# Attention operands of a tuned layer kernel as two fp16 halves, kept in memory after the first batch

## The reference

```
q, k, v = x@Wq+bq, x@Wk+bk, x@Wv+bv        # 16 heads of 128; q times 128**-0.5
q, k    = rotary(q), rotary(k)
attn    = softmax(q k^T under a causal mask)
x1      = layernorm(x + concat(attn v) @ Wo + bo)
y       = silu(x1@Wg * sg) * (x1@Wu * su)  # Wg, Wu, Wd int8, 1024 wide
out     = layernorm(x1 + (y@Wd) * sd)
```

## Time and profile before

| | |
|---|---|
| median of 3 runs | 1857.92 us (1856.61 to 1859.83) |
| the profiled execution | 1852.92 us, its span 1851.1 us |
| PE, PEld busy | 95%, 76% |
| DVE, ACT, POOL busy | 85%, 79%, 75% |
| TensorE granted clock, mean | 0.991 |

### The profile page before, as it was taken

The page is one execution under the profiler, slowest core; times in us unless marked ns, Lnnn a source line. Parts: engine busy times, 40 slices in busy tenths (PEclk is TensorE's granted clock), DMA queues, the critical chain, the costliest instruction groups (busy, mean ns, idle before and its releaser), DMA issues. The chain is left out here.

```text
span 1851.1 us, 33747 instructions
## 1 busy us (share of the span) xinstructions
PE 1755.6 (95%) x10464; PEld 1409.7 (76%) x10464; DVE 1564.9 (85%) x3748; ACT 1463.9 (79%) x2658; POOL 1394.8 (75%) x1293
## 2 busy tenths in 40 slices
PE   6899999999999999999999999999999999899997
PEld 4677877777777777777777777777777777668886
DVE  6788888888888888988888888888888889867886
ACT  5788888888888888888888888888888888754443
POOL 4688877778777878888778878787888877624554
PEclk9899999999999999999999999999999999989999
DMA  3756565666665666576666655675666765540001
GB/s 93 165 116 113 111 139 117 122 131 129 118 119 120 142 120 115 114 157 119 120 122 117 138 111 116 141 141 121 119 114 116 156 141 109 104 99 12 24 24 35
DMA packets 638257, 210.01 MB, mean 113 GB/s; under 512 B 609408, under 2 KB 622208, under 8 KB 636672
## 3 DMA queue, kind: packets, MB, share of 16 engines
q1 hardware_dynamic: 614400, 165.91, 47.9%
q10 hardware_dynamic: 23680, 41.95, 7.9%
HBM read 48.40 MB, written 8.39 MB: 31 GB/s over the span
## 5 line engine op out<-in xcount | busy, mean ns | idle before, releaser
L863 DVE SCALAR_TENSOR_TENSOR planes<-S,recip,planes 128x128 f16<-128x128 f32 (+7 forms) x512 | 417.5, 815 | 113.0 <-ACT planes L665 111.3
L656 ACT ACTIVATE S<-p_row,neg_max 128x128 f32<-128x128 f32 (+7 forms) x512 | 381.5, 745 | 138.9 <-DVE neg_max L853 138.8
L665 ACT ACTIVATE planes<-S,recip 128x128 f16<-128x128 f32 (+7 forms) x512 | 378.9, 740 | 101.4 <-DVE recip L914 73.7
L427 POOL TENSOR_TENSOR swap<-swap,sin_t 128x512 f32<-128x512 f32 x256 | 331.5, 1295 | 166.0 <-ACT swap L673 164.9
L853 DVE CUSTOM_DVE_ANT_0 p_row<-S,mask_row 128x128 f32<-128x128 f32 (+7 forms) x512 | 387.0, 756 | 27.0 <-PE S L1123 26.4
L421 POOL TENSOR_TENSOR rot<-rot,swap 128x512 f32<-128x512 f32 x252 | 325.5, 1292 | 53.6 <-DVE rot L904 50.7
L673 ACT ACTIVATE swap<-S,bqk 64x512 f32<-64x512 f32 x512 | 350.8, 685 | 18.6 <-PE S L1141 5.8
L1123 PE MATMUL S<-QKA 128*128 128x512 f32 (+4 forms) x1152 | 261.9, 354 | 10.3 <-DVE planes L863 5.7
L1123 PE MATMUL S<-QKB 128*128 128x512 f32 (+4 forms) x1152 | 260.4, 353 | 0.4 <-DVE planes L863 0.3
L1074 PE MATMUL O<-PT,VA 128*128 128x512 f16 (+3 forms) x1152 | 215.4, 328 | 29.0 <-issue 25.5
L1074 PE MATMUL O<-PT,VB 128*128 128x512 f16 (+3 forms) x1152 | 214.9, 327 | 29.4 <-issue 27.0
(11 more groups left out here) (134 smaller groups left out, 2955.5 us busy)
## 6 DMA issues: line engine op xcount, KB each, us to landing
w_raw<-in_w_heads ACTq DMA_DIRECT2D x64, 256.0 KB, 2.9
wv_raw<-in_w_heads ACTq DMA_DIRECT2D x32, 256.0 KB, 3.4
PT<-planes SPq DMA_TRANSPOSE x512, 3.4
wo_raw<-in_wo_heads ACTq DMA_DIRECT2D x32, 256.0 KB, 2.6
attn_d<-resid ACTq DMA_DIRECT2D x4, 1024.0 KB, 6.3
x_raw<-in_x_cols SPq DMA_DIRECT2D x3, 1024.0 KB, 5.9
...
```

What stands on the lines that cost most here:

```text
L427: nc.gpsimd.tensor_tensor(swap[:, c, :], swap[:, c, :], sin_t[:, half], ALU.mult).then_inc(sin_done, 1)
L656: nc.scalar.activation(row_psum(n, s)[:, 0:cols], p_row[:, k % 2, 0:cols], ACT.Exp, bias=neg_max[:, s:s + 1], scale=-1.0, accum_out=row_su ...
L665: nc.scalar.activation(row_halves(n, s)[:, 0], row_psum(n, s)[:, 0:cols].rearrange("p (j q) -> p j q", q=P), ACT.Copy, scale=recip[:, s:s ...
L863: nc.vector.scalar_tensor_tensor(halves_of[:, 1], row_psum(n, s)[:, 0:cols].rearrange("p (j q) -> p j q", q=P), recip[:, s:s + 1], halves_ ...
```

## The change

fp32r goes from x, W, WV, QK, OT and WO; they become fp16 in two halves, scaled so that they lie well inside fp16's range. The scales are computed from the data, in this way: a maximum on DVE, a sum over partitions on PE (a matmul with ones), a reciprocal on DVE. For W, WV and WO that is done in the first batch only, one weight at a time, and the finished halves are stored to DRAM (w_d, wv_d, wo_d); from the second batch on they are loaded from there, with no work on them. What depends on x (V's bounds, biases, factors) is computed once a batch for all heads. In the first batch GpSimd also multiplies each raw weight by its scale. x is scaled by ACT and DVE in the first batch, by GpSimd in the others. From the second batch on ACT copies groups 0, 1 and 2 of V, scaled, as fp32 into v_sb, and GpSimd makes both halves; group 3 stays on ACT and DVE. Large loads and stores are cut in four pieces, and the weights have two buffers each. The sum of the output becomes a multiply and add (factor pv). The feed-forward part keeps fp32r.

```diff
-    xT = sb("xT", [P, 2, KT, N], F32R)
+    xT = at(AT_X, "xT", [P, 2, KT, N])                       # fp16; W, WV, QK, OT, WO likewise
 # SP: stores of the finished halves, first batch
+                    if n < 0 and s in (4, 7) or 0 <= n < H - 2 and s == 6:
+                        keep_w(n + 2 if n >= 0 else s // 7)
 ...
 # POOL
+                    if n >= H and n < HEADS - 1 and par == 0 and s in POOL_V0:     # {4: 1, 5: 2}
+                        v_halves(n_pair(n, par), POOL_V0[s])
+                    if n >= H - 1 and n < HEADS - 2 and par == 1 and s in POOL_V1: # {7: 0}
+                        v_halves(n_pair(n, par), POOL_V1[s])
-                    if s == 0 and n >= 1 and n + 2 < HEADS:
-                        w_low(n + 2, par, 0)
-                        w_low(n + 2, par, 1)
+                    if 0 <= n < H - 3 and s == 5:
+                        w_scale(n + 3)
+                    if 1 <= n < H - 2 and s == 3:
+                        w_low(n + 2, 0)
+                        w_low(n + 2, 1)
+                    if n % H == H - 3 and n < HEADS - H and s >= 6:
+                        b, half = n // H + 1, s - 6
+                        pool.wait_ge(x_scaled, 2 * b + 2)
+                        nc.gpsimd.tensor_scalar(halves(x_raw, None, half), halves(x_raw, None, half),
+                                                sx[:, b % 2:b % 2 + 1], None, ALU.mult).then_inc(x_up, 1)
+            def v_halves(pair, i):
+                whole, tiles = v_sb[:, i, :].rearrange("p (t c) -> p t c", t=2), slice(2 * i, 2 * i + 2)
+                k = 3 * (pair - H // 2) + i + 1
+                pool.wait_ge(v_hi, 4 * pair + i + 1)
+                pool.wait_ge(attended, n_att(2 * pair - 3, 1, 7))
+                nc.gpsimd.tensor_copy(V[pair % 2][:, 0, tiles, :], whole).then_inc(vp_hi, 1)
+                pool.wait_ge(vp_hi, k)
+                nc.gpsimd.tensor_tensor(V[pair % 2][:, 1, tiles, :], whole, V[pair % 2][:, 0, tiles, :],
+                                        ALU.subtract).then_inc(vp_lo, 1)
 # ACT
-            w_high(0, 0, 0)
-            x_high(0, 0)
+            w_high(0, 0)              # waits for W's scale
+            w_high(0, 1)
+            x_high(0, 0)              # waits for x's scale, which waits for all of x
+                    if H - 3 <= n < HEADS - 3 and s == 7:
+                        load_w_halves(n + 3)
+                if in_sb(pair, i):    # pair >= 8 and i < 3
+                    wait(act, vp_lo, 3 * (pair - H // 2 - 1) + i + 1)
+                    nc.scalar.activation(v_sb[:, i, :], X[:, :], ACT.Copy, scale=of_pair(v_up, pair)).then_inc(v_hi, 1)
+                    return
 # DVE
-                    if par == 1 and s == 5 and makes_v(n + 1):
-                        weigh((n + 3) >> 1)
+                    if 0 <= n < H - 3 and s == (1 if n else 2):
+                        weigh_w(n + 3)                      # a maximum over 128x512
+                    if 0 <= n < H - 3 and s == 4:
+                        scale_w(n + 3)                      # four small operations; take_w, one more, ahead
+                    if par == 0 and s == 1 and own and n // 2 + 1 < H // 2:
+                        scale_v(n // 2 + 1)                 # three small ones; take_v, two more, ahead
+                    if par == 1 and s == 5 and (n + 3) // 2 < H // 2:
+                        weigh_v((n + 3) // 2)
+                    if par == 1 and s == 2 and own and n < H:
+                        weigh_wo(n // 2)                    # a maximum over 128x512
+                    if par == 1 and s == 5 and own and n < H:
+                        scale_wo(n // 2)                    # two small ones; take_wo, one more, ahead
+                    if n % H == H - 4 and 0 < n < HEADS - H and s == 3:
+                        weigh_all(n // H + 1)
+                    if n % H == H - 3 and 0 < n < HEADS - H and s == 1:
+                        scale_x(n // H + 1)                 # for all heads of the next batch
+                if in_sb(pair, i):                          # value_low
+                    return
-                nc.vector.tensor_tensor(into, into, X[:, :], ALU.add).then_inc(added, 1)
+                stt(into, X[:, :], of_pair(pv, pair), into, ALU.mult, ALU.add).then_inc(added, 1)
 # PE
+                        v_free(pe, n_v(n, par, i) - 1)      # in_sb groups: waits for ACT's copy, not for DVE
```

705 lines of the change are left out of this document (504 added, 201 removed).

## The result

The changed kernel takes **1841.3 us** (median of 4 runs, 1839.9 to 1844.7), the kernel before on the same chip 1857.3 (4 runs, 1856.0 to 1859.8): ratio 0.992, 95% interval 0.990 to 0.994. That is 16 us faster where 55 were forecast.

A forecast was written before the change was run, and what follows sets the result against it. The prediction took PE to bound the kernel: 1851.1 - 85 (steady heads) + 14 (batch 0) + 7 (opening) + 8 (boundaries) = 1795 us of span, 1797 as a time, 1802 as the median. The range was 1758 to 1855.

The forecast's parts named there:

- the likeliest case: Whole kernel: the forecast itself holds, median 1802 us, own range 1780 to 1828, chance 0.50.
- So PE sets the pace, but nobody is far behind: Kernel before: PE, busy 95% of the span, bounds it; DVE, ACT and POOL follow at 40 to 44 of 50 us.
- fp16's 1.7 us: PE, every head: matmul columns at the fp16 instead of the fp32r rate save 1.7 us, bounds 1.5 and 2.0.
- The term of the steady heads: Heads 16 to 62: 23.0 us a head instead of 24.8, -85 us over 47 heads, bounds -66 and -108.
- the wait in slot 0: PE ahead of a head's first attend: the wait stays, mean 0.7 us a head against 1.0 before.
- the 0.2 put down for GpSimd: From batch 1 on: low half of chunk 1 just in time or slightly late behind V's halves, 0.2 us a head.
- Rival (B): Even runs: GpSimd's V halves make the low half of chunk 1 2 us late, +47 us, 1849 us; chance 0.20.
- Rival (D): POOL: fp16 operations cost more than fp32's, deciding from 15% dearer on, 1887 us at 20%; chance 0.13.
- Batch 0: First batch: DVE's added maxima and small operations lengthen 13 heads by 1.1 us each, +14 us, bounds -10 and +33.
- Opening: Before the first scores: maxima, small operations and two matmuls for the scales add 7 us, bounds 3 and 12.
- Boundaries: Between batches: POOL's scaling of x and DVE's small operations lose 3, 3 and 2 us, +8, bounds 0 and 20.
- signs of being wrong: PE waiting for POOL, POOL's fp16 rows off 0.61 and 1.29, batch 0 over 27 us a head, boundaries over 5 each.

The follow-up runs named there:

- 6: Kernel before with ACT's high parts of the weights cut to a few columns, later heads' weights stale: 1851.3 us, ratio 0.9997 to the kernel before.
- 10: Kernel before with the third product of every projection chunk left out, PE 1.85 us a head less: 1828.8 us, ratio 0.9855 to the kernel before.
- 11: Kernel before with both cuts, ACT's high parts of the weights and the third product of every chunk: 1819.2 us, ratio 0.9801 to the kernel before.
- 4: Changed kernel with a constant as the mask's factor instead of one read from SBUF, scores scaled wrongly: 1832.1 us, ratio 0.9889 to the kernel before.
- 5: Changed kernel with all V halves made on ACT and DVE again, GpSimd's part left out: 1844.9 us, ratio 0.996 to the kernel before.
- 17: Changed kernel with batch 0's bv copies on ACT, and later even heads' output projection in slot 2, V's last group in 4: 1857.6 us, ratio 1.0016.
- 12: Changed kernel with batch 0's weight maxima on DVE taken over four columns, scales no longer maxima: 1835.3 us, ratio 0.989 to the kernel before.
- 13: Changed kernel with GpSimd's batch 0 weight scalings cut to a few columns, weights left unscaled: 1847.3 us, ratio 0.9965 to the kernel before.

## Why the prediction was wrong

The sign was right and the size was not: -55 us forecast, -16 measured. That is inside the wide range, and outside the likeliest case's own.

**The step that failed** is the first one, "So PE sets the pace, but nobody is far behind", with what follows from it: that fp16's 1.7 us comes off every head, and that of DVE and ACT "neither becomes the bound". A busy share of 95% made me take the other engines' shares for slack. What the runs show: PE held stretch O, and in stretch E the rows were as long (6: ACT lighter alone 0; 10: PE lighter alone 0.03 us off E, 1.25 off O; 11: both, 0.45 and 1.25). So PE's relief is worth 0.64 us a head at 1.85 less work, not all of it; with ACT's relief 0.85. The page had a hint: DVE waited for PE's scores only 26 us in the whole run of before, 0.4 a head. It is a hint and no bound, since 0.64 came back.

**The term of the steady heads.** Forecast 24.8 - 1.7 - 0.3 + 0.2 = 23.0; measured 23.75. PE's own work fell as forecast, by 1.84 us (forecast 1.7), to 22.12. The term that was mis-sized is the wait in slot 0: put at 0.7, it is 1.63 in the mean (1.14 and 2.11, medians of heads 20 to 43). That is 0.93 too much, less the 0.2 put down for GpSimd, which did not come. Before the change the same medians are 1.25 and 0.45, in the mean 0.85; the forecast's 1.0 was read from one head of each kind. That DVE's three operations "take 910.76 - 907.81 = 2.95 us and do not change" is true, but I let them start when PE's scores of row 7 are there. They start when the ring of rows gets there, 1.6 us later in the even runs (scores done 969.25, mask 970.81). 47 heads x 1.05 are -49 us, and boundaries and last heads +9.

**The mask's factor** was not priced at all: 0.06 us x 8 rows, 0.47 us a head of DVE, of which 0.16 to 0.19 reach the end (4): 7 to 9 us.

**GpSimd.** The forecast expected "little from the move itself": right, 0.3 us of 1133 (5). Rival (B) did not happen: where a new pair begins, in the odd runs, V's halves are done 3.5 us ahead of the attend, and PE does not wait at the first scores of head 37 (at 970.39; the low half of chunk 1 was done at 968.64). Rival (D), dearer fp16, was wrong in sign: subtractions with fp16 operands take 1.16 us, not 1.29, casts 0.61 as before. The term of +0.2 us a head for this chain was thus not needed. The scalings however took 1.57 to 1.62 us a 512-wide weight, where the text had "0.61 to 1.29", and 2.85 per half of x.

**Batch 0**: +14 forecast, +21.6 measured. Even heads 26.0 are as said, odd ones 27.4. That DVE holds the odd heads is supported (17: 1.26 us less when 2.0 us of copies leave DVE), but not alone: DVE is busy for 25.9 us of an odd head's 27.4, not for 26.8 as two expectations have it, and GpSimd for 25.9 too. Not foreseen was that DVE's small work collides with GpSimd's: `ident` grew from 0.21 to 0.72 us by its place alone. The Trainium skill's SBUF — State Buffer (Who interferes with whom), which I cited for 0.57 us, states the rule at work here; I used it for the price of three instructions, not for the place of all. Not foreseen either was that PE waits for transposes in four of these heads. How the remaining difference divides between maxima, scalings, collisions and stores stays open: cutting either of the first two moved collisions about (12, 13).

**Opening** +9.2 for +7, within its bounds. **Boundaries**: heads 16 to 63 cost 17.2 us over 47 steady ones, 7.9 before, +9.3 for +8. It fits by luck in part: only some 7 of them lie around the three boundaries, the others in heads 59 to 62 (5.9 us over the steady ones, 1.9 before), for which the forecast has no term. **Tail**: -3.9 for 0; the other kernels with the same tail show 239 to 244, so it is scatter.

**Slips in the sums**: 6528 columns at 0.417 ns are 2.7 us, not 2.8; a head's 52,224 columns are 21.8 us at that pitch, not 22.1; rival (D) at 20% comes to 1884 by its own terms, not 1887. None of them carries the miss.

**Lines that were to show it**: chunks at 216 ns, DVE under 86% (85.6 of a pair) and batch 0 with DVE above 90% (93) came true. Two heads took 47.5 us and not 46, POOL was at 82% and not near 88, and the first scores stood at 34.4 and not near 32. Two of the signs of being wrong showed: odd heads of batch 0 over 27 us, and one boundary (heads 43 to 48) 5.4 us over its steady heads. None of them asked the question that decided, how long the rows alone would take.
